# Another order of the row matmuls within a turn of a fused attention kernel, with the halves of the array alternating

## What is computed

```python
def _L0_attn_ref(x, W_qkv, b_qkv):          # x: (2, 4096, 256), 16 heads
    qkv = (x @ W_qkv + b_qkv).reshape(B, D, 3, H, p).transpose(2, 0, 3, 1, 4)
    q, k, v = (qkv[0], qkv[1], qkv[2])
    scores = jax.nn.softmax(jnp.einsum('bhip,bhjp->bhij', q, k), axis=-1)
    out = jnp.einsum('bhij,bhjp->bhip', scores, v)
    return out.reshape(B, D, N)
...
def _L0_ffn_ref(x, ...):
    h = jnp.einsum('bsd,dh->bsh', x, W_exp) + b_exp
    h = butterfly(h, up_weights, D_HIDDEN)
    h = jax.nn.gelu(h + up_bias, approximate=False)
    h = butterfly(h, down_weights, D_HIDDEN)
    y = jnp.einsum('bsh,hd->bsd', h, W_con) + b_con
    return y + down_bias
x = L0_attn_x
xn = _layernorm(x, axis=-1)
x = x + _L0_attn_ref(xn, ...) + _L0_ffn_ref(xn, ...)
```

## Time and profile before

| what | value |
| --- | --- |
| median of 3 runs | 5672.61 us |
| lowest, highest | 5670.88, 5674.43 us |
| the profiled execution, its own time | 5674.86 us |
| its span, first to last instruction | 5673.1 us |
| mean granted TensorE clock, share of full speed | 0.992 |
| TensorE busy | 5605.1 us (99%) |
| ScalarE busy | 4977.2 us (88%) |
| VectorE busy | 4884.6 us (86%) |
| GpSimd busy | 524.8 us (9%) |

### The profile page before, as it was taken

One profiled execution on the slowest core, in us unless ns is written; L12 is line 12 of the kernel. 1 busy time (PEld: TensorE's weight loads), 2 busy tenths in 40 slices (PEclk: granted clock), 3 DMA queues, 4 the chain that ended last, 5 costly groups with the idle time before them and its releaser, 6 DMA issues. The chain is left out here.

```text
span 5673.1 us, 97332 instructions
## 1 busy us (share of the span) xinstructions
PE 5605.1 (99%) x35880; PEld 2613.5 (46%) x35880; DVE 4884.6 (86%) x9104; ACT 4977.2 (88%) x9651; POOL 524.8 (9%) x482
## 2 busy tenths in 40 slices
PE   8799999999999999999999999999999999999999
PEld 5444444444444444444444444444444444444698
DVE  6689999999999999999999999999999999996233
ACT  3489999999999999999999999999999999999544
POOL 2245564000000000000000000000000000000000
PEclk9889999999999999999999999999999999999999
DMA  8611111000000000000000000000000000000111
GB/s 288 200 43 43 50 54 42 21 21 19 14 16 21 21 21 21 15 21 21 21 18 14 16 21 21 21 20 16 21 21 21 17 12 20 21 21 2 34 44 41
DMA packets 232761, 197.02 MB, mean 35 GB/s; under 512 B 171752, under 2 KB 192616, under 8 KB 220520
## 3 DMA queue, kind: packets, MB, share of 16 engines
q1 hardware_dynamic: 228848, 168.00, 10.4%
q0 software_dynamic: 3456, 23.07, 1.4%
HBM read 128.07 MB, written 60.82 MB: 33 GB/s over the span
## 5 line engine op out<-in xcount | busy, mean ns | idle before, releaser
L646 ACT ACTIVATE probs<-psum 128x512 f32<-128x512 f32 x8192 | 4222.6, 608 | 294.8 <-PE psum L843 292.8
L708 DVE TENSOR_REDUCE maxima<-psum 128x1 f32<-128x512 f32 x6036 | 3966.7, 686 | 364.7 <-PE psum L821 255.6
L821 PE MATMUL psum<-k_rows,q_rows 48*128 48x512 f32 x7042 | 2494.3, 455 | 0.6 <-ACT spill L670 0.6
L857 PE MATMUL psum<-probs,v_cols 128*32 128x512 f32 x16384 | 2184.7, 605 | 0.5
L843 PE MATMUL psum<-q_rows,k_rows 50*128 50x512 f32 x8192 | 2061.2, 424 | 0.0
L821 PEld LDWEIGHTS psum<-k_rows,q_rows 48*128 48x128 f32 x7042 | 1176.6, 184 | 1248.8 <-DVE maxima L704 809.6
L843 PEld LDWEIGHTS psum<-q_rows,k_rows 50*128 50x128 f32 x8192 | 1266.5, 186 | 135.0 <-ACT probs L646 44.5
L704 DVE CUSTOM_DVE_ANT_0 merged<-psum,spill 128x512 bf16<-128x512 f32 x1006 | 684.8, 681 | 2.7 <-issue 1.9
L670 ACT ACTIVATE spill<-psum 128x512 f32<-128x512 f32 x1006 | 601.0, 597 | 23.9 <-PE psum L821 23.6
L857 PEld LDWEIGHTS psum<-probs,v_cols 128*32 128x32 f32 x16384 | 323.3, 108 | 622.0 <-issue 325.8
L821 PEld LDWEIGHTS psum<-k_diff,q_rows 48*128 48x128 f32 x1006 | 184.6, 183 | 843.0 <-DVE maxima L708 787.7
(11 more groups left out here) (94 smaller groups left out, 2067.0 us busy)
## 6 DMA issues: line engine op xcount, KB each, us to landing
q_rows<-q_parts SPq DMA_DIRECT2D x128, 256.0 KB
q_parts<-parts SPq DMA_DIRECT2D x32, 512.0 KB, 6.0
k_parts<-parts SPq DMA_DIRECT2D x32, 512.0 KB, 3.7
k_rows<-k_parts SPq DMA_DIRECT2D x64, 256.0 KB
q_rows<-q_parts SPq DMA_DIRECT2D x128, 128.0 KB
planes<-in_up_planes POOLq DMA_DIRECT2D x10, 1024.0 KB, 11.3
planes<-in_down_planes POOLq DMA_DIRECT2D x10, 1024.0 KB, 5.4
y<-in_x SPq DMA_DIRECT2D x16, 512.0 KB, 6.0
```

Source lines behind the costliest of these rows:

```text
L646: nc.scalar.activation(probs[:, 2 * (u % 2) + half, BANK * g:BANK * g + BANK], ps_s[:, r % 4, :], ACT.Exp).then_inc(s_exp, 1)
L708: nc.vector.tensor_reduce(largest, region(use), axis=AX_X, op=ALU.max).then_inc(s_region_free, 1)
L821: nc.tensor.matmul(region(use_of[n, j]), q_rows[m % 4][lower:lower + ROWS, P * t:P * t + P], keys[lower:lower + ROWS, :], start=True, stop ...
L857: last = nc.tensor.matmul(ps_o[VW * g:VW * g + VW, :], v_cols[:, KT * (head % 2) + UNITS * half + at, :], probs[:, 2 * (u % 2) + half, BAN ...
```

## The change

Three things are set anew, and nothing is added or taken out. First, the order of a turn: p0 p1 p2, s0 to s3, p3 p4, sums of half 1, p5, s4 s5, p6 p7, s6 s7, sums of half 0. Second, `PIECE` and `SCORE`: with the half behind each, the turn is now

p0(1) p1(0) p2(1) s0(1) s1(0) s2(1) s3(0) p3(1) p4(0), sums of half 1, p5(0) s4(1) s5(0) p6(1) p7(0) s6(1) s7(0), sums of half 0.

So the nine row matmuls stand before the first sums of the turn. Third, the difference is p0 and belongs to the turn's own tile; the relu stands ahead of the eight exps, and VectorE reduces p1 to p7. The waits follow from the same rotation: p3 waits for the relu of p0, p4 for the reduce of p1, p6 for that of p3, p7 for that of p4, and p2 for that of the last turn's p7.

```diff
-        PIECE = [(1, 0), (1, 1), (0, 0), (1, 2), (0, 1), (0, 2), (1, 3), (0, 3)]
-        DIFFERENCE, MERGED = 3, 6
+        PIECE = [(1, 2), (0, 0), (1, 0), (1, 1), (0, 1), (0, 2), (1, 3), (0, 3)]
+        DIFFERENCE, MERGED = 0, 6
...
-        SCORE = [(r // 2 % 2, 2 * (r // 4) + r % 2) for r in range(2 * QG)]
+        SCORE = [(1 - r % 2, r // 2) for r in range(2 * QG)]
...
                 for u in range(UNITS_ALL):
+                    if u + AHEAD < TILES_ALL:
+                        rectify(u + AHEAD)
                     if u + 1 < UNITS_ALL:
-                        for r in range(QG):
-                            exp(u + 1, r)
-                    if u + AHEAD + 1 < TILES_ALL:
-                        rectify(u + AHEAD + 1)
-                    if u + 1 < UNITS_ALL:
-                        for r in range(QG, 2 * QG):
+                        for r in range(2 * QG):
                             exp(u + 1, r)
...
-                    piece(n, 0)
-                    score(u + 1, 0)
-                    piece(n, 1)
-                    score(u + 1, 1)
-                    score(u + 1, 2)
-                    piece(n, 2)
-                    score(u + 1, 3)
-                    sums(u, 0)
+                    for j in range(3):
+                        piece(n, j)
+                    for r in range(QG):
+                        score(u + 1, r)
                     piece(n, 3)
                     piece(n, 4)
+                    sums(u, 1)
+                    piece(n, 5)
                     score(u + 1, 4)
                     score(u + 1, 5)
-                    piece(n, 5)
+                    piece(n, 6)
+                    piece(n, 7)
                     score(u + 1, 6)
                     score(u + 1, 7)
-                    piece(n, 6)
-                    piece(n, 7)
-                    sums(u, 1)
+                    sums(u, 0)
```

More of the change, by code:

```diff
@@ L466, in attention_and_butterfly_ffn @@
                         use((n, what, pair), what == "second")
-        use((PAIRED, DIFFERENCE), False)
         for n in range(PAIRED, TILES_ALL + TURN_TILE + 1):
@@ L471, in attention_and_butterfly_ffn @@
             for j in range(PIECES if n < TILES_ALL else 0):
[L472 to L475, removed]
+                use((n, j), j != DIFFERENCE)
         vector_uses, scalar_uses = list(accumulate(by_vector)), list(accumulate(by_scalar))
@@ L643, in exp @@
                     if g == 0 and u >= 2:
-                        act.wait_ge(s_pv, 2 * (u - 2) + half + 1)
+                        act.wait_ge(s_pv, 2 * (u - 2) + 2 - half)
                     act.wait_ge(s_score, 2 * QG * u + r + 1)
@@ L678, in _ @@
                 act.wait_ge(s_ones_in, 16 * 4)
-                for r in range(QG):
-                    exp(0, r)
-                rectify(AHEAD)
-                for r in range(QG, 2 * QG):
+                for r in range(2 * QG):
                     exp(0, r)
                 for u in range(UNITS_ALL):
+                    if u + AHEAD < TILES_ALL:
+                        rectify(u + AHEAD)
                     if u + 1 < UNITS_ALL:
-                        for r in range(QG):
-                            exp(u + 1, r)
-                    if u + AHEAD + 1 < TILES_ALL:
-                        rectify(u + AHEAD + 1)
-                    if u + 1 < UNITS_ALL:
-                        for r in range(QG, 2 * QG):
+                        for r in range(2 * QG):
                             exp(u + 1, r)
@@ L807, in piece @@
                 def piece(n, j):
-                    if j == DIFFERENCE:
-                        n += 1
                     if n >= TILES_ALL:
@@ L850, in sums @@
                     head = s // 2
-                    if at == 0 and half == 0:
+                    if at == 0 and half == 1:
                         if s > 0:
@@ L858, in sums @@
                                                 probs[:, 2 * (u % 2) + half, BANK * g:BANK * g + BANK],
-                                                start=(at == 0 and half == 0), stop=(at == UNITS - 1 and half == 1))
+                                                start=(at == 0 and half == 1), stop=(at == UNITS - 1 and half == 0))
                     last.then_inc(s_pv, 1)
@@ L866, in _ @@
                         pairs(n, i)
-                piece(PAIRED - 1, DIFFERENCE)
                 for n in range(PAIRED, AHEAD):
```

## The result

| | before | after |
| --- | --- | --- |
| median | 5672.61 us (7 runs, 5668.83 to 5674.64) | 5693.51 us (7 runs, 5689.39 to 5694.44) |
| ratio | | 1.0035, 95% interval 1.0025 to 1.0046 |
| span of the profiled execution | 5673.1 us | 5691.7 us |
| mean granted clock | 0.992 | 0.992 |

The change makes the kernel 21 us slower; 28 were forecast (5700).

The account below looks back on a forecast made before the run. Bound: a turn's closed chain of 4.86 us through TensorE rows and VectorE's reduce, left unchanged; two special turns in 16 add 0.48 us, 62 times, taken as 28 us: 5700 us, own range 5687 to 5712, 8 in 10 within 5668 to 5732.

Parts of the forecast that it names:

- the two special places: Once in 16 turns each, the sums' transpose and the end of the maxima: together 0.48 us more, 62 times.
- the maxima's end: Once in 16 turns, VectorE's small operations and TensorE's transpose of the maxima: +0.51 us against +0.22 before, 0.29 more.
- The pacing wait: Long part's last row p4 waits for VectorE's reduce of p1; turn stays 4.86 us, same as before: 0.
- The transpose of the sums: Once in 16 turns, it runs before p1's reduce: +0.31 us against +0.12 before, 0.19 more.
- The chain: One turn's closed sequence through the second piece, its VectorE reduce, the waiting last row and both sums: 4.86 us.
- The sum: Special turns' 0.19 + 0.29 = 0.48 us, 62 times: about 30 us, bounds 15 to 40, 28 taken.
- Alternating halves: New order of array halves in both parts; fuller half keeps five and four rows, so no gain: 0.
- the prediction's own sum for p7: Short part: p7's load possible at 3.13 us after p4's reduce, needed by 3.21; slack 0.08.
- Longer ordinary turns: Rival: p4's reduce ends 0.05 us beyond its slack in each of 1003 turns: 5750 us; chance 0.10.
- no difference: Rival: VectorE's pause and shorter reduces absorb the special turns, or ordinary turns win 0.03 us: 5673 us; chance 0.15.
- Strict order as the pace: Rival: the halves' program order spaces the last rows, 0.235 us less in 1003 turns: 5464 us; chance 0.08 together.

Follow-up runs that it names:

- The first experiment: The changed kernel with the scores' halves in pairs (1,1,0,0) instead of alternating: 5822.17 us, ratio 1.0264 to the kernel before.

## Why the prediction was right, and where it was off

**The direction and its reason.** Ordinary turns unchanged and the whole loss in the two special places of 16 turns was the forecast, and three quarters or more of the loss lie there (15 us). Moving the maxima's end away took back 16 of 21 us; that run shows that such turns can be bought back, not that the maxima's end had lost so much. The share of the sums' transpose is read from its turns alone.

**The pacing wait.** "Same as before: 0" holds to 0.005 us a turn. VectorE's times in an ordinary turn came out within 0.03 of those laid out. The 0.005 in the short part were not foreseen and are 2 to 5 us of the 21; their cause is open (with pairs in the long part only, the sum of 16 turns is 0.04 lower).

**The transpose of the sums.** Said +0.31 against +0.12, measured +0.25 against +0.12. The chain's +0.25 was exact. The further 0.03 to 0.09 for p7 did not come: p4's reduce ends only 0.10 later in the short part than in an ordinary turn, and the slack is 0.11.

**The maxima's end.** Said +0.51 against +0.22, measured 0.355 against 0.235. This is the term that was mis-sized. I had "put" the first small operation "at the same" 0.18 as the reduce over the maxima; the rows above show 0.18 for the latter (3031.83 to 3032.00, rounded) but only 0.07 for the former (3032.60 to 3032.67). Before, VectorE was waiting for TensorE at that point, and the distance was that wait. And the slack was 0.11, not 0.08. So p7 came 0.15 late, not 0.27. In the next turn p1's load was 0.19 late, not 0.24 with its head.

**The sum.** 0.33 in 16 turns against 0.48 laid out, and 0.45 in the 28 us taken. The special places alone give 0.25, half of what was laid out: 0.06 too much for the transpose of the sums, 0.17 for the maxima's end. That 28 stands so near to 21 is in part luck: the 0.08 of the ordinary turns (by the medians), not foreseen, make up for a third of these two errors.

**Alternating halves.** The forecast "No gain: 0" is true of this change, but "a part lasts as long as its fuller half" holds only while every load on that half comes in time. The first experiment kept the fuller halves and made p7 the second row on its half instead of the third, and its wait for p4's reduce, which had a slack of 0.11, cost 0.13 in every turn. The new order would have cost 150 us with the scores in pairs, instead of 21. So the short part's order does matter in the changed kernel, for a reason that the prediction's own sum for p7 holds (due time less 0.10, against the end of p4's reduce) and that I did not redo for the first experiment. Strict program order would have given 5929 us there; the run took 5822, with p7 ahead of p6, and in the earlier trace rows the scores s6 and s7 start ahead of p5. The Trainium skill ("TensorE: Matmul & The Clock Gate", Part 3: Packing small matmuls) states that matmuls start and end strictly in program order. For the starts of row matmuls on different halves these traces do not agree.

**The rivals.** Longer ordinary turns did not come; two and four memsets show how near they were. That p1's reduce starts 0.03 sooner, the last ground for "no difference", was tried by its reverse: the 0.03 belong to the second place in the queue, and the change kept the pacing piece in it. Strict order as the pace is excluded by the old order with its scores alternating, which would have gained 236 us by it and gained nothing, and by p7's start ahead of p6.

## What to carry to other kernels

When every engine is busy nine tenths of the time, write down the closed chain of one turn, with each wait's slack, before reordering anything: a new order that leaves the chain as it was has nothing to win there, and may lose by moving rare work in front of it. Put occasional operations behind the reduce that has a pause after it, and issue first, of two instructions that start together, the one whose consumer the chain runs through. Before moving rows between the halves of the array, work out for each row with a wait when it is due on its own half: the same load at 0.37 was in time for the third row of a half and 0.13 us late for the second.

## What the runs showed of the hardware that was not expected

- Of two row matmuls loaded 0.004 us apart on different halves, the second is answered 0.03 us later, whichever engine waits for it (0.57 and 0.53 before; 0.57 and 0.54 with the order exchanged). In a chain passed 1003 times that is 30 us.
- A weight load that comes when its half has nothing to run costs more than its own lateness: the next row on that half starts 0.34 us behind instead of 0.235. For p7 in pairs 0.03 of lateness became 0.13 us a turn (5822 against 5693 us).
- A load can go ahead of another that waits for its own half: s2's at 3004.41 before s1's at 3004.65, in the old order with alternating scores.
- A small operation on VectorE costs the reduces behind it less than its own length: 0.16 us of cast between two reduces moved the second by 0.07, and two memsets with 0.17 us of busy time moved the third reduce behind by 0.08.
